# Rounding the third expert's high halves on VectorE instead of ScalarE, with three more slots for them

## The chip, the cores and the metric

The kernel runs on one core of one Trainium2 chip. The metric is the device time of one execution, in microseconds (us). Lower is better. Engines are named as in the profile: PE is TensorE (PEld its weight loads), DVE is VectorE, ACT is ScalarE, POOL is GpSimd, SP issues the DMAs.

## The reference, cut to what matters

The input x has the shape (32, 56, 56, 96), f32. Two residual layers follow each other:

```
x = x + attention(norm(x))         # shifted 7x7 windows, 12 heads, relative bias, masks
t = tokens of x
scores -> softmax over 4 experts, the best 2 kept and renormalised     # "masked"
h = gelu(norm(t) @ w1[e] + b1[e])      # e = 0..3, 96 -> 384
y = h @ w2[e] + b2[e]                  # 384 -> 96
out = t + sum over e of masked[e] * y[e]
```

All four experts are computed for all tokens; the gate sets two of them to zero. The change is in the second matmul of the experts, `h @ w2[e]`, and in how h is prepared for it.

## The kernel before

An image is cut into four units of 784 tokens (two strips of 7 by 56), 128 units in all. The 31 first images run in a loop whose body holds four units, the last image stands behind it. Each engine has a program of its own, written out by hand, and engines meet only at semaphores. The sequence within an engine is fixed by the code: nothing reorders it.

A step of the loop works on three units at once: f, whose expert layer is done; a, whose attention is done; b, whose norm, queries, keys and values are prepared. In f's first stretch, called the gelu stretch here, PE computes the hidden layer in 24 pieces (`hidden`), and ACT takes each through the gelu (`gelus`) into `g_sb`, 12 chunks of 128 hidden features by 784 tokens in f32. Three chunks make an expert. In the second stretch PE runs the attention of a in eight rounds n = 0 to 7 and puts the twelve groups of the experts' second matmul (`experts(f, g)`, three groups for each expert) in between: `GROUPS_AT` says which group stands in which round (0, 1, 2 in round 0, group 3 in round 1, 4 in round 2, 5 in round 3, 6 in round 5, 7 in round 6), and `LATE_GROUPS` those that follow the rounds.

The matmul reads h as two f16 halves. The high half `g_hi` is the rounded chunk, the low half `g_lo` is the difference between `g_sb` and it. Both have six slots, so that a chunk of the third or fourth expert takes the slot of a chunk of the first or second one, once `y_done` tells that its groups are through.

- Chunks 0 to 5: DVE rounds them in the gelu stretch (line 875), behind the router's arithmetic. The low halves of 0 to 2 are DVE's (line 880), those of 3 to 11 are POOL's (line 450).
- Chunks 6 to 11: ACT rounds them (line 536) in the rounds of the attention that the table `ROUND_AT` names: 6, 7, 8 in rounds 1, 2, 3, behind `copy_pt(n)` and `exps(n + 1)`.
- DVE's next work behind chunk 5 is `softmax_pair(a, 0)`: the maximum over the first scores (line 737) and their subtraction (line 741). ACT takes the exponential (line 560), PE transposes it (line 1038), ACT copies it to SBUF (line 565), PE multiplies it by the values (line 1055).
- POOL's program of a unit: low halves 3 to 5, three additions (line 460) of gated expert outputs to `xr`, the norm of b (lines 423, 428, 433), low halves 6 to 8 with an addition behind each, the others.

Groups 3 to 5 wait in PE for the low halves of chunks 3 to 5 (`lo_done`), groups 6 to 8 for those of chunks 6 to 8.

Of the kernel before, what the change touches and what calls it, by code (L numbers as in the profile page):

```python
# [28 lines left out]
F16 = mybir.dt.float16  # L29
ALU = mybir.AluOpType  # L30
ACT = mybir.ActivationFunctionType
AX = mybir.AxisListType

B, IMG, C = 32, 56, 96
# [7 lines left out]
CHUNKS = EXPERTS * HID // 128  # L42
CPE = HID // 128
UPI = 4
STRIP = W * IMG
TOK = 2 * STRIP
# [10 lines left out]
def at(unit, per_unit, k=0):  # L57

    m, c = unit
    return m * (UPI * per_unit) + (c * per_unit + k)  # L60
# [43 lines left out]
PARTS = len(GROUP_TILES)  # L104
# [1 line left out]
COMBINES_AT = ((0, 1), (2,), (3,), (4,), (5,), (), (6,), (7,))  # L106
LATE_GROUPS = (8, 9, 10, 11)
STATS_AT = ((), (0, 1), (2, 3), (4, 5, 6), (), (), (), ())
ROUND_AT = ((), (6,), (7,), (8,), (), (9,), (10,), (11,))


T1_AT = 4
# [11 lines left out]
N_XV = 8  # L124
N_PROJ, N_T2, N_H, N_Y = 2, 2, 24, PARTS * EXPERTS
N_XHI, N_X1LO = 4, 4
N_ROUND, N_LO = CHUNKS // 2, CHUNKS - CPE
PAD = 16
N_STACK = 16 * 3 * GROUPS
N_SPREAD = 16 * 3 * GH  # L130
# [10 lines left out]
def build(nc, x, packed, wp, consts, out, keys):  # L141
    ctx = ExitStack()
    with ctx:
        def sb(name, shape, dt=F32):
            return ctx.enter_context(nc.sbuf_tensor(name, shape, dt))
# [84 lines left out]
        gden = sb("gden", [LANES, W])  # L230
        gate = sb("gate", [LANES, W * EXPERTS])
        g_sb = sb("g_sb", [128, CHUNKS, TOK])
        g_hi = sb("g_hi", [128, 2 * CPE, TOK + PAD], F16)
        g_lo = sb("g_lo", [128, 2 * CPE, TOK + PAD], F16)
        y_gated = sb("y_gated", [LANES, 4, 3 * C])

# [172 lines left out]
        def _(pool):  # L409
# [32 lines left out]

            def low_part(f, chunk):

                if chunk < 2 * CPE:
                    pool.wait_ge(hi_dve, at(f, N_ROUND, chunk + 1))
                else:
                    pool.wait_ge(hi_act, at(f, N_ROUND, chunk - 2 * CPE + 1))
                slot = chunk % (2 * CPE)
                nc.gpsimd.tensor_tensor(g_lo[:, slot, 0:TOK], g_sb[:, chunk, :], g_hi[:, slot, 0:TOK],  # L450
                                        ALU.subtract).then_inc(lo_done, 1)

            def add(f, u, g):
# [40 lines left out]
        def _(act):  # L494
# [38 lines left out]
            def round_chunk(f, chunk):  # L533

                act.wait_ge(y_done, at(f, N_Y, PARTS * (chunk // CPE - 1)))
                nc.scalar.activation(g_hi[:, chunk - 2 * CPE, 0:TOK], g_sb[:, chunk, :], ACT.Copy  # L536
                                     ).then_inc(hi_act, 1)

            def gelus(f, k0):
# [75 lines left out]
            def step(f, a, b, u):  # L615
                for i in range(8):
                    gelus(f, 3 * i)
                    if i == 0:
                        router_tanh(f)
                if a is not None:  # L620
                    load_tables(ACT.Exp)
                    attention(a, b, f)
                else:
                    for chunk in range(2 * CPE, CHUNKS):
                        round_chunk(f, chunk)

            schedule(act, step, prologue)
# [3 lines left out]
        def _(dve):  # L631
# [310 lines left out]
            def step(f, a, b, u):  # L942
                router_b(f)
                for chunk in range(CPE):
                    round_chunk(f, chunk)
                for chunk in range(CPE):
                    low_part(f, chunk)
                for chunk in range(CPE, 2 * CPE):
                    round_chunk(f, chunk)
                if a is not None:  # L950
                    softmax_pair(a, 0)
                    attention(a, b, f)
                else:
                    for g in range(N_Y):
                        combine(f, g)
# [5 lines left out]
        def _(pe):  # L961
# [143 lines left out]
            def experts(f, g):  # L1105

                e, j0, n = tiles_of(g)
                if e == 0:
                    pe.wait_ge(lo_dve, at(f, CPE, CPE))
                else:  # L1110
                    pe.wait_ge(lo_done, at(f, N_LO, CPE * e))
                if g < 3:
                    pe.wait_ge(gelu_done, at(f, N_H, N_H - 2 + g))
                earlier = [i for i in range(g) if Y_BANK[i] == Y_BANK[g]]
                if earlier:
                    pe.wait_ge(gated, at(f, N_Y, max(earlier) + 1))
                y = y_bank(g)[:, 0:n * C]
                T.matmul(y, ones16[:, :], b2_16[:, e * 3 * C:e * 3 * C + n * C], start=True, stop=False,
                         skip_group_check=True)
                for k in range(n):  # L1120
                    cols = slice((j0 + k) * LANES, (j0 + k) * LANES + 128)
                    for c in range(CPE):
                        slot, wc = e % 2 * CPE + c, slice((e * CPE + c) * C, (e * CPE + c + 1) * C)
                        outp = y[:, k * C:(k + 1) * C]
                        T.matmul(outp, g_hi[:, slot, cols], w2_hi[:, wc], start=False, stop=False,  # L1125
                                 skip_group_check=True)
                        T.matmul(outp, g_hi[:, slot, cols], w2_lo[:, wc], start=False, stop=False,  # L1127
                                 skip_group_check=True)
                        ins = T.matmul(outp, g_lo[:, slot, cols], w2_hi[:, wc], start=False,  # L1129
                                       stop=(c == CPE - 1), skip_group_check=True)  # L1130
                ins.then_inc(y_done, 1)

# [145 lines left out]
```

## Time and profile before

| | |
|---|---|
| median of 3 runs | 6519.17 us (6518.93 to 6523.38) |
| the profiled execution, its own time | 6518.15 us |
| its span | 6516.3 us |
| granted TensorE clock | 0.995 |
| PE busy | 6280.1 us, 96% |
| DVE busy | 5032.7 us, 77% |
| ACT busy | 4717.1 us, 72% |
| POOL busy | 3756.0 us, 58% |

1.85 us of the time lie around the span. A unit takes some 50 us: the span over 128 units is 50.9. PE has the highest busy share, in all 40 slices of the span, but its records overlap and their ends are modelled, so that the share alone does not say that nothing else is waited for. In a row of the timeline, the figures are the start, the duration, and in brackets how long the engine had stood idle before it and what ended that. Rows that are merged (x3) can overlap: an instruction of DVE starts before the one ahead of it has ended.

### The profile page before, as it was taken

The page shows a single profiled execution, that of the slowest core. Times are in us where ns is not written, and L with a number is a line of the kernel's source. Part 1 is how long each engine was busy: PE and PEld are TensorE (multiplying, and loading weights), DVE is VectorE, ACT ScalarE, POOL GpSimd, SP SyncE. Part 2 cuts the span into 40 slices and gives each one's busy share as a digit, 9 for nine tenths or more (in the row PEclk, how much of TensorE's full clock was granted, in tenths as well). Part 3 has the DMA queues.
Part 4 walks back from the last instruction along what each step waited for, and adds up shares of the span by engine and source line. Part 5 has one row for each costly group of instructions (what it writes and reads, how often), then busy time and mean ns, then how long its engine had stood idle before and what let it go on. Part 6 is the DMA issues. An engine that isn't in the chain of part 4 may idle for free.

```text
span 6516.3 us, 265099 instructions
## 1 busy us (share of the span) xinstructions
PE 6280.1 (96%) x99456; PEld 5077.8 (78%) x99456; DVE 5032.7 (77%) x15655; ACT 4717.1 (72%) x9087; POOL 3756.0 (58%) x3337
## 2 busy tenths in 40 slices
PE   5999999999999999999999999999999999999998
PEld 4788778777877787778777877787787778777876
DVE  5777777777777777777777777777777777777775
ACT  3777777777777777777777777777777777777775
POOL 2565556555655565556556555655565556555655
PEclk9999999999999999999999999999999999999998
DMA  1111111111111111111111111111111111111110
GB/s 58 45 43 45 46 45 43 44 47 45 45 44 46 44 45 45 46 44 45 45 46 43 45 46 45 43 45 46 45 44 44 46 45 43 45 47 44 45 43 22
DMA packets 190611, 290.00 MB, mean 45 GB/s; under 512 B 42450, under 2 KB 151634, under 8 KB 189266
## 3 DMA queue, kind: packets, MB, share of 16 engines
q1 hardware_dynamic: 189394, 273.23, 14.5%
q8 instruction: 831, 13.62, 0.9%
q14 instruction: 386, 3.16, 0.2%
HBM read 138.18 MB, written 77.07 MB: 33 GB/s over the span
## 4 chain that ended last, share of the span: by engine, by line
PE 76%; DVE 13%; ACT 4%; issue 3%; POOL 2%; SPq 1%; DVEq 0%; DMA 0%; ACTq 0%; POOLq 0%
PE ps_t L1038 12%; PE ps_o L1055 10%; PE ps_f L966 8%; PE ps_f L967 8%; PE ps_f L968 8%; PE ps_s L1018 5%; PE ps_s L1028 4%; PE ps_f L1129 4%; PE ps_f L1127 4%; PE ps_f L1125 4%; POOL rstd L439 2%; PE ps_o L1064 2%; DVE stat L768 2%; PE ps_f L1070 2%; PE ps_t L985 2%
## 5 line engine op out<-in xcount | busy, mean ns | idle before, releaser
L450 POOL TENSOR_TENSOR g_lo<-g_sb,g_hi 128x784 f16<-128x784 f32 x1152 | 2013.5, 1756 | 1720.7 <-DVE g_hi L875 1019.1
L543 ACT ACTIVATE g_sb<-ps_f 128x392 f32<-128x392 f32 x3072 | 1525.5, 497 | 128.9 <-PE ps_f L968 127.8
L565 ACT ACTIVATE pt_sb<-ps_t 113x588 f32<-113x588 f32 x1024 | 676.2, 660 | 1011.2 <-PE ps_t L1038 998.2
L737 DVE TENSOR_REDUCE s_max<-ps_s 113x12 f32<-113x588 f32 x1024 | 789.2, 771 | 655.9 <-PE ps_s L1028 651.6
L1129 PE MATMUL ps_f<-w_hi,g_lo 128*128 128x96 f16 x8832 | 1229.1, 206 | 0.0
L1127 PE MATMUL ps_f<-w_lo,g_hi 128*128 128x96 f16 x8832 | 1228.5, 206 | 0.0
L1125 PE MATMUL ps_f<-w_hi,g_hi 128*128 128x96 f16 x8832 | 1227.9, 206 | 0.0
L460 POOL TENSOR_TENSOR xr<-y_gated,xr 112x192 f32<-112x192 f32 (+1 forms) x1536 | 985.3, 659 | 370.2 <-DVE y_gated L893 271.3
L966 PE MATMUL ps_f<-x_hi,w_hi 128*128 128x392 f16 x3072 | 1012.4, 330 | 19.8 <-issue 5.3
L967 PE MATMUL ps_f<-x_lo,w_hi 128*128 128x392 f16 x3072 | 1010.9, 329 | 0.0
L968 PE MATMUL ps_f<-x_hi,w_lo 128*128 128x392 f16 x3072 | 1010.9, 329 | 0.0
L1038 PE MATMUL ps_t<-ident,p_sb 113*113 113x113 f32 x6144 | 854.3, 275 | 26.8 <-ACT p_sb L560 26.6
L1127 PEld LDWEIGHTS ps_f<-w_lo,g_hi 128*128 128x128 f16 x8832 | 863.8, 98 | 10.3
L1125 PEld LDWEIGHTS ps_f<-w_hi,g_hi 128*128 128x128 f16 x8832 | 865.9, 98 | 0.1
L1129 PEld LDWEIGHTS ps_f<-w_hi,g_lo 128*128 128x128 f16 x8832 | 864.3, 98 | 0.0
L741 DVE TENSOR_TENSOR s_sub<-ps_s,s_max 113x588 f32<-113x588 f32 x1024 | 790.5, 772 | 57.0
L1055 PEld LDWEIGHTS ps_o<-v_bd,pt_sb 113*49 113x49 f32 x24576 | 737.5, 125 | 114.2 <-ACT pt_sb L565 67.0
L1055 PE MATMUL ps_o<-v_bd,pt_sb 113*49 113x18 f32 x24576 | 785.1, 198 | 23.9 <-ACT pt_sb L565 20.1
L560 ACT ACTIVATE p_sb<-s_sub 113x588 f32<-113x588 f32 x1024 | 715.6, 699 | 78.2 <-DVE s_sub L741 72.9
L1038 PEld LDWEIGHTS ps_t<-ident,p_sb 113*113 113x113 f32 x6144 | 695.6, 178 | 80.2 <-issue 51.3
L536 ACT ACTIVATE g_hi<-g_sb 128x784 f16<-128x784 f32 x768 | 647.0, 843 | 3.1 <-PE ps_f L1129 3.1
L439 POOL TENSOR_TENSOR rstd<-ve,cst 112x4 f32<-112x4 f32 (+1 forms) x256 | 270.6, 1057 | 596.6 <-DVE ve L777 596.6
(132 smaller groups left out, 13418.1 us busy)
## 6 DMA issues: line engine op xcount, KB each, us to landing
k_bd<-keys SPq DMA_DIRECT2D x1536, 36.8 KB
q_st<-qk_hi SPq DMA_DIRECT2D x768, 49.0 KB, 1.9
xr<-x SPq DMA_DIRECT2D x224, 139.1 KB
out<-xr SPq DMA_DIRECT2D x224, 139.1 KB
xa<-x SPq DMA_DIRECT2D x224, 136.5 KB
keys<-qk_hi SPq DMA_DIRECT2D x128, 147.0 KB, 2.4
keys<-qk_lo SPq DMA_DIRECT2D x128, 147.0 KB, 2.8
q_st<-qk_lo SPq DMA_DIRECT2D x384, 49.0 KB, 2.0
```

What stands on the lines that cost most here:

```text
L450: nc.gpsimd.tensor_tensor(g_lo[:, slot, 0:TOK], g_sb[:, chunk, :], g_hi[:, slot, 0:TOK], ALU.subtract).then_inc(lo_done, 1)
L460: nc.gpsimd.tensor_tensor(slot, y_gated[:, g % 4, 0:n * C], slot, ALU.add).then_inc(comb_done, 1)
L543: nc.scalar.activation(g_sb[:, chunk, half * STRIP:(half + 1) * STRIP], h_bank[k % 3][:, 0:STRIP], ACT.Gelu, scale=1.0 / WSCALE).then_inc( ...
L741: V.tensor_tensor(s_sub[:, n % 2, :, 0:WW], scores, s_max[:, :].unsqueeze(2).broadcast_to([SPAN, HEADS, WW]), ALU.subtract).then_inc(sub_d ...
L966: T.matmul(outp, lhs_hi, rhs_hi, start=start, stop=False, skip_group_check=True)
L967: T.matmul(outp, lhs_hi, rhs_lo, start=False, stop=False, skip_group_check=True)
L968: return T.matmul(outp, lhs_lo, rhs_hi, start=False, stop=True, skip_group_check=True)
L1038: ins = T.transpose(bank[2 + p // 4][0:SPAN, (p % 4) * 128:(p % 4) * 128 + SPAN], p_sb[0:SPAN, n % 2, 2 * p:2 * p + 2, :].rearrange("p h k ...
L1055: ins = T.matmul(ps_o[NB * s:NB * s + WW, O0 + p * 2 * VW:O0 + (p + 1) * 2 * VW], pt_sb[0:SPAN, p, s * WW:(s + 1) * WW], v_bd[0:SPAN, win ...
L1125: T.matmul(outp, g_hi[:, slot, cols], w2_hi[:, wc], start=False, stop=False, skip_group_check=True)
L1127: T.matmul(outp, g_hi[:, slot, cols], w2_lo[:, wc], start=False, stop=False, skip_group_check=True)
L1129: ins = T.matmul(outp, g_lo[:, slot, cols], w2_hi[:, wc], start=False, stop=(c == CPE - 1), skip_group_check=True)
```

## The change

DVE rounds chunks 6, 7 and 8 as well, behind chunk 5 and ahead of the first maximum. `g_hi` grows from six slots to nine, so that these three overwrite nothing that the first expert still reads; `g_lo` keeps six. ACT's table loses the entries of the chunks 6, 7 and 8, and chunks 9 to 11 now take the slots 0 to 2 of `g_hi`. POOL's low halves of 6 to 8 wait for DVE's rounding and, on their own now, for the groups of the expert whose `g_lo` slot they take. PE's and SP's programs have the same rows as before.

```diff
-ROUND_AT = ((), (6,), (7,), (8,), (), (9,), (10,), (11,))
+ROUND_AT = ((), (), (), (), (), (9,), (10,), (11,))
-N_ROUND, N_LO = CHUNKS // 2, CHUNKS - CPE
+N_ROUND, N_LO = 3 * CPE, CHUNKS - CPE
-        g_hi = sb("g_hi", [128, 2 * CPE, TOK + PAD], F16)
+        g_hi = sb("g_hi", [128, 3 * CPE, TOK + PAD], F16)
 # POOL, low_part
-                if chunk < 2 * CPE:
+                if chunk < 3 * CPE:
                     pool.wait_ge(hi_dve, at(f, N_ROUND, chunk + 1))
                 else:
-                    pool.wait_ge(hi_act, at(f, N_ROUND, chunk - 2 * CPE + 1))
+                    pool.wait_ge(hi_act, at(f, CPE, chunk - 3 * CPE + 1))
+                if chunk >= 2 * CPE:
+                    pool.wait_ge(y_done, at(f, N_Y, PARTS * (chunk // CPE - 1)))
                 slot = chunk % (2 * CPE)
-                nc.gpsimd.tensor_tensor(g_lo[:, slot, 0:TOK], g_sb[:, chunk, :], g_hi[:, slot, 0:TOK],
+                nc.gpsimd.tensor_tensor(g_lo[:, slot, 0:TOK], g_sb[:, chunk, :],
+                                        g_hi[:, chunk % (3 * CPE), 0:TOK],
                                         ALU.subtract).then_inc(lo_done, 1)
 # ACT, round_chunk
-                nc.scalar.activation(g_hi[:, chunk - 2 * CPE, 0:TOK], g_sb[:, chunk, :], ACT.Copy
+                nc.scalar.activation(g_hi[:, chunk - 3 * CPE, 0:TOK], g_sb[:, chunk, :], ACT.Copy
                                      ).then_inc(hi_act, 1)
 # ACT, step, last unit only
-                    for chunk in range(2 * CPE, CHUNKS):
+                    for chunk in range(3 * CPE, CHUNKS):
                         round_chunk(f, chunk)
 # DVE, step
-                for chunk in range(CPE, 2 * CPE):
+                for chunk in range(CPE, 3 * CPE):
                     round_chunk(f, chunk)
 # PE, experts: the same matmuls, other slots of g_hi
-                        slot, wc = e % 2 * CPE + c, slice((e * CPE + c) * C, (e * CPE + c + 1) * C)
+                        hi, lo = e % 3 * CPE + c, e % 2 * CPE + c
+                        wc = slice((e * CPE + c) * C, (e * CPE + c + 1) * C)
```

On DVE, in the loop's body between the low halves of the first expert and the first maximum of the attention, before:

```order
L880 TENSOR_TENSOR g_lo<-g_sb,g_hi 128x784 [waits hi_dve]
L874 REGISTER_ALU
L875 CAST g_hi<-g_sb 128x784 [waits gelu_done]
L874 REGISTER_ALU
L875 CAST g_hi<-g_sb 128x784 [waits gelu_done]
L874 REGISTER_ALU
L875 CAST g_hi<-g_sb 128x784 [waits gelu_done]
L736 ISA
L737 TENSOR_REDUCE s_max<-ps_s 113x12 [waits s_done]
L740 REGISTER_ALU [waits max_done]
L741 TENSOR_TENSOR s_sub<-ps_s,s_max 113x12x49 [waits exp_done]
```

The same place after:

```order
L878 REGISTER_ALU
L879 CAST g_hi<-g_sb 128x784 [waits gelu_done]
L878 REGISTER_ALU
L879 CAST g_hi<-g_sb 128x784 [waits gelu_done]
L878 REGISTER_ALU
L879 CAST g_hi<-g_sb 128x784 [waits gelu_done]
L740 ISA
L741 TENSOR_REDUCE s_max<-ps_s 113x12 [waits s_done]
L744 REGISTER_ALU [waits max_done]
L745 TENSOR_TENSOR s_sub<-ps_s,s_max 113x12x49 [waits exp_done]
```

The casts shown last are those of the chunks 6, 7 and 8; three like them, of 3 to 5, stand ahead of them. Six casts in a row now stand ahead of the first maximum where there were three.

On ACT, in rounds 1 and 2 of the attention, before:

```order
L565 ACTIVATE pt_sb<-ps_t 113x588 [waits pt_done]
L554 REGISTER_ALU
L560 ACTIVATE p_sb<-s_sub 113x12x49 [waits pt_done,sub_done]
L535 REGISTER_ALU
L536 ACTIVATE g_hi<-g_sb 128x784 [waits y_done]
L564 REGISTER_ALU
L565 ACTIVATE pt_sb<-ps_t 113x588 [waits pt_done]
```

and after:

```order
L569 ACTIVATE pt_sb<-ps_t 113x588 [waits pt_done]
L558 REGISTER_ALU
L564 ACTIVATE p_sb<-s_sub 113x12x49 [waits pt_done,sub_done]
L568 REGISTER_ALU
L569 ACTIVATE pt_sb<-ps_t 113x588 [waits pt_done]
```

The rounding is gone from between the exponential of one round and the copy of the next one.

## Rows read from the trace of the kernel before

**Rows 1.** The page's chain that ended last, by engine.
```profile
PE 76%; DVE 13%; ACT 4%; issue 3%; POOL 2%; SPq 1%; DVEq 0%; DMA 0%; ACTq 0%; POOLq 0%
```

**Rows 2.** Waits: engine, tile, line <- releaser: us in total, times, longest.
```profile
PE ps_t L1038 <- ACT p_sb L560: 26.6, 125, 1.1
PE ps_o L1055 <- ACT pt_sb L565: 20.1, 128, 0.6
```

**Rows 3.** ACT's timeline in rounds 1 to 4 of a unit.
```profile
3032.27 0.70 ACT L560 ACTIVATE p_sb<-s_sub 113x588 f32<-113x588 f32 x1
3032.86 0.84 ACT L536 ACTIVATE g_hi<-g_sb 128x784 f16<-128x784 f32 x1
3034.76 0.66 ACT L565 ACTIVATE pt_sb<-ps_t 113x588 f32<-113x588 f32 x1 [1.05 <-PE ps_t L1038]
...
3037.64 0.66 ACT L565 ACTIVATE pt_sb<-ps_t 113x588 f32<-113x588 f32 x1 [0.90 <-PE ps_t L1038]
...
3040.94 0.66 ACT L565 ACTIVATE pt_sb<-ps_t 113x588 f32<-113x588 f32 x1 [1.32 <-PE ps_t L1038]
```

**Rows 4.** Groups by line, ACT and DVE: count, busy us, mean ns, idle before.
```profile
L536 ACT ACTIVATE g_hi<-g_sb 128x784 f16<-128x784 f32 x768 | 647.0, 843 | 3.1 <-PE ps_f L1129 3.1
...
L875 DVE CAST g_hi<-g_sb 128x784 f16<-128x784 f32 x768 | 388.9, 563 | 16.3
L880 DVE TENSOR_TENSOR g_lo<-g_sb,g_hi 128x784 f16<-128x784 f32 x384 | 350.7, 969 | 0.0
```

**Rows 5.** DVE's timeline from the casts to the first subtraction, same unit.
```profile
3018.45 2.74 DVE L880 TENSOR_TENSOR g_lo<-g_sb,g_hi 128x784 f16<-128x784 f32 x3
3021.10 1.51 DVE L875 CAST g_hi<-g_sb 128x784 f16<-128x784 f32 x3
3025.03 0.77 DVE L737 TENSOR_REDUCE s_max<-ps_s 113x12 f32<-113x588 f32 x1 [2.41 <-PE ps_s L1028]
3025.92 0.77 DVE L741 TENSOR_TENSOR s_sub<-ps_s,s_max 113x588 f32<-113x588 f32 x1
```

**Rows 6.** The chain from the first scores to the first transpose, same unit.
```profile
3025.03 0.78 DVE s_max L737
3025.87 0.04 issue
3025.92 0.78 DVE s_sub L741
3026.76 0.05 issue
3026.81 0.71 ACT p_sb L560
3027.52 0.14 issue
3027.65 0.82 PE ps_t L1038 x6
```

**Rows 7.** DVE's first maximum, the units with the shortest and longest idle.
```profile
326.73 0.77 DVE L737 TENSOR_REDUCE s_max<-ps_s 113x12 f32<-113x588 f32 x1 [2.16 <-PE ps_s L1028]
...
6426.79 0.77 DVE L737 TENSOR_REDUCE s_max<-ps_s 113x12 f32<-113x588 f32 x1 [2.69 <-PE ps_s L1028]
```

**Rows 8.** ACT's gelus of the same unit.
```profile
3014.45 10.44 ACT L543 ACTIVATE g_sb<-ps_f 128x392 f32<-128x392 f32 x21
```

**Rows 9.** POOL's low halves 3, and 4 and 5, same unit.
```profile
3021.74 2.41 POOL L450 TENSOR_TENSOR g_lo<-g_sb,g_hi 128x784 f16<-128x784 f32 x1 [7.88 <-DVE g_hi L875]
...
3024.11 3.31 POOL L450 TENSOR_TENSOR g_lo<-g_sb,g_hi 128x784 f16<-128x784 f32 x2
```

**Rows 10.** POOL's additions behind them, in the unit with the shortest idle.
```profile
2322.55 5.69 POOL L450 TENSOR_TENSOR g_lo<-g_sb,g_hi 128x784 f16<-128x784 f32 x3 [8.45 <-DVE g_hi L875]
2330.07 1.90 POOL L460 TENSOR_TENSOR xr<-y_gated,xr 112x192 f32<-112x192 f32 x3 [1.83 <-DVE y_gated L893]
```

**Rows 11.** PE at the start of group 3, round 1.
```profile
3031.51 0.25 PE L1118 MATMUL ps_f<-b,ones 128*128 128x192 f16 x1
```

**Rows 12.** POOL's timeline in the last unit.
```profile
6474.68 5.67 POOL L450 TENSOR_TENSOR g_lo<-g_sb,g_hi 128x784 f16<-128x784 f32 x3 [7.75 <-DVE g_hi L875]
6480.31 1.89 POOL L460 TENSOR_TENSOR xr<-y_gated,xr 112x192 f32<-112x192 f32 x3
6482.16 1.67 POOL L450 TENSOR_TENSOR g_lo<-g_sb,g_hi 128x784 f16<-128x784 f32 x1
...
6494.32 0.59 POOL L460 TENSOR_TENSOR xr<-y_gated,xr 112x192 f32<-112x192 f32 x1
6495.36 1.34 POOL L460 TENSOR_TENSOR xr<-y_gated,xr 112x288 f32<-112x288 f32 x2 [0.45 <-DVE y_gated L893]
...
6498.33 0.79 POOL L460 TENSOR_TENSOR xr<-y_gated,xr 112x288 f32<-112x288 f32 x1 [0.78 <-DVE y_gated L893]
```

More of the change, by code:

```diff
@@ L1122, in experts @@
                     for c in range(CPE):
-                        slot, wc = e % 2 * CPE + c, slice((e * CPE + c) * C, (e * CPE + c + 1) * C)
+                        hi, lo = e % 3 * CPE + c, e % 2 * CPE + c
+                        wc = slice((e * CPE + c) * C, (e * CPE + c + 1) * C)
                         outp = y[:, k * C:(k + 1) * C]
-                        T.matmul(outp, g_hi[:, slot, cols], w2_hi[:, wc], start=False, stop=False,
+                        T.matmul(outp, g_hi[:, hi, cols], w2_hi[:, wc], start=False, stop=False,
                                  skip_group_check=True)
-                        T.matmul(outp, g_hi[:, slot, cols], w2_lo[:, wc], start=False, stop=False,
+                        T.matmul(outp, g_hi[:, hi, cols], w2_lo[:, wc], start=False, stop=False,
                                  skip_group_check=True)
-                        ins = T.matmul(outp, g_lo[:, slot, cols], w2_hi[:, wc], start=False,
+                        ins = T.matmul(outp, g_lo[:, lo, cols], w2_hi[:, wc], start=False,
                                        stop=(c == CPE - 1), skip_group_check=True)
```

## The prediction, on record before the result was known

> **What bounds the kernel now.** I read the chain that ended last first: 76% of it is PE, 13% DVE, 4% ACT [rows 1]. ACT loses work by this change, so the question is whether any of its 4% lies where the roundings stood. The table of waits comes next: PE stood idle for ACT's exponential 26.6 us and for ACT's copy 20.1 us, each about once in a unit (125 and 128 times) [rows 2]. Then the timeline of one unit shows where. The reader is to see two things in it. In rounds 1 to 3 it is ACT that waits for PE: behind each rounding it stands idle 1.05, 0.90 and 1.32 us before PE's transposes release it [rows 3]. And at the first scores, ahead of round 0, the chain runs over DVE and ACT with no gap to speak of: maximum, subtraction, exponential, transposes, from 3025.03 to 3027.65 [rows 6]. There a microsecond on DVE is a microsecond of the unit, and that is the place in front of which the change puts its three casts.
>
> **The change part by part.**
>
> ACT loses 3 roundings in each of 128 units, 384 x 0.843 = 323.7 us busy [rows 4]. All of it lies beside PE's work: if the rounding goes, ACT's idle time behind it grows from 0.90 to 1.32 us to some 1.7 to 2.2 us, and the copy starts when it started before. Gain on the path: nothing. The upper bound of a gain is what PE waits for ACT at all, 26.6 + 20.1 = 46.7 us [rows 2]; but the first of these waits is the transpose of round 0 (3027.65, behind the chain of rows 6), where no rounding stood ahead, and the second one's count is one in a unit where six or more roundings are done. I take 0 and keep 46.7 as the far end of a gain.
>
> DVE gets 3 casts in each unit. Their form is that of the other six: 563 ns each [rows 4], and three of them in 1.51 us, so one every (1.51 - 0.56)/2 = 0.475 us [rows 5]. Three more are 1.43 us in a row. Their input: 21 gelus run from 3014.45 to 3024.89, one every 0.497 us, behind three earlier ones [rows 8]. Chunks 6, 7 and 8 need 14, 16 and 18 gelus: done at 3014.45 + 11, 13, 15 x 0.497 = 3019.9, 3020.9 and 3021.9. DVE is free for them at 3022.53, 3023.00 and 3023.48, so none waits. The last ends at 3022.61 + 1.43 = 3024.04, and the first maximum, which waits for PE's scores, starts at 3025.03 [rows 5]. Cover: DVE's idle time of 2.41 us there, of which 0.98 is left. It is not the same in each unit: of the 127 first maxima that follow the casts the idle time is 2.16 at the least and 2.69 at the most [rows 7], their sum is 310.6 us (mean 2.45). In the worst, 0.73 us is left. Cost: 0. If the cover were gone, each missing 0.1 us would be 0.1 x 127 = 12.7 us.
>
> The bounds of a cast here: 0.475 us a piece from below, the row of the same operation; from above the nearest slower row on DVE of the same size, the low half, three in 2.74, one every (2.74 - 0.97)/2 = 0.885 us [rows 4, 5]. Three of those are 2.66 us: 0.50, 0.25 and 0.07 us too many for the units with an idle time of about 2.16 (30 units), 2.41 (32) and 2.59 and more (65). Sum 15.0 + 8.0 + 4.6 = 27.6 us. I take the lower bound, since operation, types and shape are its own and slots 6 to 8 lie at the same stride as the others.
>
> POOL pays for the casts, though it has no new work. Its low half of chunk 3 takes 2.41 us beside the casts of chunks 4 and 5, while the next two take 3.31 us together [rows 9]. Counted back from its end (3024.15) by the undisturbed 1.67 us [rows 12], it did its work from 3022.48 on, which is when DVE was through with its last cast (3022.61 less the overlap). With three casts more in the same row, POOL is held until 3022.48 + 1.43 = 3023.9, and its low halves end at 3027.42 + 1.43 = 3028.85. Who waits: group 3 of the experts starts at 3031.51 [rows 11], 2.66 us later; the additions wait for DVE anyway, 1.83 us at the least, so 0.40 us is left to them [rows 10]. Behind them POOL's program runs as before, and low half 6 starts when the norm of b is done, not when its rounding is. Cost in the loop: 0.
>
> The last unit is the one place where POOL is on the path. Its rows follow each other without a gap from 6474.68 to 6494.9, and the additions and groups behind them hang on the last low half [rows 12]. ACT's roundings are not awaited there (low half 6 starts as the additions end), so their removal gives nothing, and POOL's delay shifts everything to the end: +1.43 us. Lower bound 0, if the waits further down take up some of it.
>
> The other edits go together: POOL's added wait for `y_done` names groups that are done before (ACT waited for the same ones), and what stands behind it is an addition that was behind it already; three more slots' margins in one memset of the setup; PE and SP run the rows that they ran. Cost 0.
>
> Sum against the profiled execution: 6518.15 + 0 (ACT) + 0 (DVE) + 0 (POOL in the loop) + 1.43 (last unit) = 6519.6 us. The median of the runs shown, 6519.17, lies 1.0 above that execution, so the two differ by no more than runs do. The span should be 6516.3 + 1.4 = 6517.7.
>
> What the Trainium skill says of this place ("SBUF — State Buffer", section "Who interferes with whom"): a cast in a two-port mode and a GpSimd instruction hold the port pair that they share for a whole instruction, and the one that issues first blocks the other fully. The trace agrees that POOL is blocked, by 2.41 - 1.67 = 0.74 us. It does not agree on who goes first: POOL's low half had started at 3021.74, ahead of the cast of chunk 5, and DVE's cast took its 0.56 us all the same (768 casts, mean 563 ns). By the page's rule one of the three new casts should find POOL in possession; by the row none does.
>
> **The rivals.**
>
> *POOL gets the port between two casts (slower).* The mechanism: POOL's waiting low half gets in at the gap behind chunk 5's cast, and DVE's next cast waits until it is through. Price: 1.67 us of delay for DVE, with 2.45 - 1.43 = 1.02 us of cover on the mean: 0.65 us late in each of 127 units, 82.6 us, and the time is 6601. It decides from the point where DVE's casts end later than PE's first scores, because exponential and transposes follow at once [rows 6]. If it happened before each new cast: 3 x 1.67 = 5.0 us against 1.02, 3.99 x 127 = 506 us, 7025. For it: POOL is pending during the whole row of casts. Against it: it was pending during the step from chunk 4's cast to 5's as well, in every unit, and lost there each time. It is also what the Trainium skill's page on SBUF would have. Chance 0.07.
>
> *The casts are as slow as the low halves (slower).* 6518.15 + 27.6 + 1.4 = 6547. For it: the longer row of casts runs beside work that the old ones did not see, the last gelus' writes to `g_sb` above all. Against it: the casts of 3 to 5 ran beside gelus and POOL and kept their duration. Chance 0.03.
>
> *ACT's relief is worth something (faster).* If PE's waits for the copy came from ACT being late by its roundings, they would go: 6518.15 - 20.1 + 1.4 = 6499.5, at most 6518.15 - 46.7 + 1.4 = 6473. For it: 20.1 us in 128 waits. Against it: rounds 1 to 3 have 0.90 us and more of idle time on ACT behind the rounding [rows 3]. Chance 0.03.
>
> **How the numbers follow.** Forecast 0.87, rivals 0.07, 0.03 and 0.03. The likeliest time is 6519.6. Within 0.2%, which is 13 us here (6506 to 6532) and about what a measurement of this kernel can tell from no change, lies the forecast: same 0.87. Slower 0.10, faster 0.03. The range: the forecast's own reaches from 6512 (0.05 us gained in each unit, an eighth of what PE waits for ACT) to 6528 (the highest of the runs shown, 6523.4, and 0.04 us lost in each unit); with it some 0.05 of the forecast and 0.13 of the rivals are left out.
>
> **What would show each step.** In the profile after: line 536's group has 384 instructions and DVE's cast 1152 at 0.56 us; DVE's idle time before the first maximum is 0.7 to 1.3 us instead of 2.16 to 2.69; POOL's low half 3 takes about 3.8 us instead of 2.41, and its idle time before the first additions falls by 1.4; ACT stands idle 1.7 us and more in rounds 2 to 4; POOL's last addition starts 1.4 us later against the span's start. The prediction is wrong if a cast lasts 2 us (POOL got in), if the first maximum follows a cast directly, or if PE's waits for `p_sb` grow or those for `pt_sb` vanish.

## The result and the profile after

| | before | after |
|---|---|---|
| median (4 runs each) | 6521.07 us | 6557.10 us |
| lowest and highest | 6518.93, 6523.38 | 6555.52, 6563.12 |
| span of the profiled execution | 6516.3 us | 6555.4 us |
| granted TensorE clock | 0.995 | 0.996 |
| DVE, ACT, POOL busy | 5032.7, 4717.1, 3756.0 | 5210.3, 4427.5, 3939.2 |

The ratio is 1.0059, interval 1.0047 to 1.0071: slower by 0.6%, outside the range of 6512 to 6528. The prediction was wrong.

First, the rows on which it rested. The groups by line, after (line, engine, operation, output and inputs, count, then busy us and mean ns, then idle before):

```profile
L453 POOL TENSOR_TENSOR g_lo<-g_sb,g_hi 128x784 f16<-128x784 f32 x1152 | 2196.7, 1916 | 1722.4 <-DVE g_hi L879 1022.7
...
L879 DVE CAST g_hi<-g_sb 128x784 f16<-128x784 f32 x1152 | 572.3, 563 | 16.3
...
L540 ACT ACTIVATE g_hi<-g_sb 128x784 f16<-128x784 f32 x384 | 323.7, 843 | 6.9 <-PE ps_f L1134 6.9
```

ACT did 384 roundings less at 843 ns, DVE 384 casts more at 563 ns, as worked out from [rows 4]. The timeline of DVE in one unit, after:

```profile
3139.86 2.95 DVE L879 CAST g_hi<-g_sb 128x784 f16<-128x784 f32 x6
3144.11 0.77 DVE L741 TENSOR_REDUCE s_max<-ps_s 113x12 f32<-113x588 f32 x1 [1.30 <-PE ps_s L1032]
```

and POOL's in the same unit:

```profile
3140.50 7.11 POOL L453 TENSOR_TENSOR g_lo<-g_sb,g_hi 128x784 f16<-128x784 f32 x3 [9.02 <-DVE g_hi L879]
```

Six casts take 2.95 us where three took 1.51 [rows 5]: 1.44 more. The first maximum still waits for PE, by 1.30 us here. POOL's three low halves take 7.11 us where they took 5.67 to 5.69 [rows 10, 12]. All of this is as forecast. What is new stands in the page's chain that ended last:

```profile
PE 75%; DVE 12%; issue 5%; ACT 4%; POOL 2%; SPq 1%; DVEq 0%; ACTq 0%; DMA 0%; POOLq 0%
```

"issue" was 3% [rows 1] and is 5% now: time in which an engine of the chain waited for nothing that the profile shows. To find its place I took the length of each unit, from one first maximum to the next, in both traces. DVE's first maxima in two units in a row, with the loop's branch between them, before:

```profile
3074.91 0.77 DVE L737 TENSOR_REDUCE s_max<-ps_s 113x12 f32<-113x588 f32 x1 [2.59 <-PE ps_s L1028]
...
3125.12 0.77 DVE L737 TENSOR_REDUCE s_max<-ps_s 113x12 f32<-113x588 f32 x1 [2.17 <-PE ps_s L1028]
```

and after:

```profile
3092.65 0.77 DVE L741 TENSOR_REDUCE s_max<-ps_s 113x12 f32<-113x588 f32 x1 [1.16 <-PE ps_s L1032]
...
3144.11 0.77 DVE L741 TENSOR_REDUCE s_max<-ps_s 113x12 f32<-113x588 f32 x1 [1.30 <-PE ps_s L1032]
```

50.21 us before, 51.46 after. The median of all of them, by place in the loop's body of four units (31 or 32 units each):

| | first | second | third | fourth, over the loop's branch |
|---|---|---|---|---|
| before | 49.89 | 49.89 | 49.89 | 50.21 |
| after | 49.89 | 50.17 | 49.89 | 51.21 |

The first and the third unit take what they took, with the same casts and the same delay of POOL in them. Summed over the trace: the fourth units grew by 32.1 us, the second ones by 7.7, the first and third together shrank by 1.9; the stretch behind the last maximum grew by 2.6 and the one ahead of the first shrank by 1.4. That is 39.1, the whole difference of the spans.

**The fourth unit.** The chain there, after (start, us, what; a "q" behind the engine's name is its sequencer, the part that reads the instructions, waits and branches):

```profile
3129.21 0.04 ACT x_hi L530
3129.25 0.32 issue
3129.57 0.05 ACTq L308
3129.62 2.38 issue
3132.00 0.03 ACTq L308
...
3132.26 0.51 ACT g_sb L547
3132.76 0.05 issue
3132.81 0.34 PE ps_f L970
```

Line 308 is the loop itself, `nc.Fori(..., hint_back_edge=True)`. Its rows around that branch, for ACT and DVE (duration min/median/max in ns, first and last start):

```profile
L308 ACTq COMPARE_BRANCH  x1: 49/49/49, 3129.6 to 3129.6; - x1
...
L308 ACTq BRANCH_PREFETCH_HINT  x1: 31/31/31, 3132.0 to 3132.0; - x1
...
L308 DVEq COMPARE_BRANCH  x1: 68/68/68, 3132.3 to 3132.3; - x1
L308 DVEq BRANCH_PREFETCH_HINT  x1: 39/39/39, 3132.8 to 3132.8; - x1
```

ACT branches back at 3129.6, and the first instruction of the body, the hint row, runs at 3132.0; the median over the 30 branches that go back is 2.18 us. DVE needs 0.53. The same two rows before:

```profile
L308 ACTq COMPARE_BRANCH  x1: 49/49/49, 3111.4 to 3111.4; - x1
L308 ACTq BRANCH_PREFETCH_HINT  x1: 31/31/31, 3111.8 to 3111.8; - x1
```

0.41 us at the median. Who waits, after (engine, tile, line <- releaser: us in total, times, longest):

```profile
ACT g_sb L547 <- PE ps_f L972: 160.7, 227, 2.7
...
DVE gden L856 <- ACT gtanh L554: 31.2, 30, 1.3
...
PE ps_f L970 <- ACT g_sb L547: 22.0, 30, 1.0
```

PE's hidden layer has no free PSUM tile until the gelus begin: 30 waits of up to 1.0 us for `g_sb` that were not there before. The first row names PE as the releaser of gelus; at this place the chain above shows ACT standing without an instruction instead, so a releaser that the profile infers can be the wrong one.

**The second unit.** DVE's second scaling of the norm, `xn`, waits for POOL's `rstd`. Chain after:

```profile
3026.79 1.11 POOL rstd L439
3027.90 0.03 issue
...
3027.95 0.40 issue
3028.35 0.47 DVE xn L792
```

and at the same place before:

```profile
3009.34 1.11 POOL rstd L439
...
3010.49 0.04 issue
3010.54 0.46 DVE xn L788
```

`rstd` is ready in both; DVE's instruction starts 0.45 us behind it instead of 0.10.

No cast and no rounding of the change runs at either place. What the two share is that an engine stands with its inputs ready. The page counts DMA packets of kind "instruction" in two queues, 831 of 16 KB in one and 386 (before) or 388 (after) of 8 KB in the other. I took as theory 1 that the changed length of ACT's and DVE's programs moves the places at which their instruction stream is interrupted (from the trace's counts, a turn of the body is 527 instructions on ACT before and 511 after, 782 and 806 on DVE; POOL's grew too, from 231 to 267, but its time from the branch to the first row is 0.21 us in both), theory 2 that ACT's missing roundings shift it badly, theory 3 that the casts, or POOL's delay by them, are what costs.

The trace also has the start of every instruction packet, and that is where theory 1 can be seen directly. In the stretch from 3129.6 to 3131.0, after, in which ACT stands at the branch:

```profile
q14 instruction: 1, 0.01, 1.4%
```

and before, from 3110.6 until ACT is through with the branch at 3111.8:

```profile
DMA packets 0, 0.00 MB, mean 0 GB/s; under 512 B 0, under 2 KB 0, under 8 KB 0
```

Read for every turn, an 8 KB packet starts 0.65 to 1.00 us behind ACT's branch (median 0.67) in all 30 turns after, and ACT's first row follows a good microsecond behind its landing. Before, none starts between the branch and the first row in any turn: the nearest one ahead of the branch lies 7.4 us from it. At the late `xn`, such a packet starts 0.67 us behind the late row in 31 of the 32 turns, and in none before. In DVE's program, before, the rows at which such packets start follow each other at a distance of 126 to 129: so 8 KB hold some 128 instructions, 64 bytes each.

### The profile page after: what moved, and what is told of

Read it like the earlier page. It is cut to its first block, busy times and chain, and to the rows that moved or that the text cites. A ratio compares the mean times of both kernels' runs of the same rounds, so it can differ in the third digit from the quotient of the medians.

```text
span 6555.4 us, 266487 instructions
## 1 busy us (share of the span) xinstructions
PE 6282.3 (96%) x99456; PEld 5072.1 (77%) x99456; DVE 5210.3 (79%) x16039; ACT 4427.5 (68%) x8703; POOL 3939.2 (60%) x3337
## 4 chain that ended last, share of the span: by engine, by line
PE 75%; DVE 12%; issue 5%; ACT 4%; POOL 2%; SPq 1%; DVEq 0%; ACTq 0%; DMA 0%; POOLq 0%
PE ps_t L1042 12%; PE ps_o L1059 10%; PE ps_f L970 8%; PE ps_f L971 8%; PE ps_f L972 8%; PE ps_s L1022 5%; PE ps_s L1032 4%; PE ps_f L1132 3%; PE ps_f L1134 3%; PE ps_f L1130 3%; POOL rstd L439 2%; PE ps_o L1068 2%; DVE stat L772 2%; PE ps_f L1074 2%; PE ps_t L989 2%
## 5 line engine op out<-in xcount | busy, mean ns | idle before, releaser
L453 POOL TENSOR_TENSOR g_lo<-g_sb,g_hi 128x784 f16<-128x784 f32 x1152 | 2196.7, 1916 | 1722.4 <-DVE g_hi L879 1022.7
L1042 PE MATMUL ps_t<-ident,p_sb 113*113 113x113 f32 x6144 | 854.0, 275 | 25.8 <-ACT p_sb L564 25.5
L1059 PE MATMUL ps_o<-v_bd,pt_sb 113*49 113x18 f32 x24576 | 784.5, 199 | 24.0 <-ACT pt_sb L569 20.1
L879 DVE CAST g_hi<-g_sb 128x784 f16<-128x784 f32 x1152 | 572.3, 563 | 16.3
```

Of the source, the lines that this page charges most:

```text
L1042: ins = T.transpose(bank[2 + p // 4][0:SPAN, (p % 4) * 128:(p % 4) * 128 + SPAN], p_sb[0:SPAN, n % 2, 2 * p:2 * p + 2, :].rearrange("p h k ...
L1059: ins = T.matmul(ps_o[NB * s:NB * s + WW, O0 + p * 2 * VW:O0 + (p + 1) * 2 * VW], pt_sb[0:SPAN, p, s * WW:(s + 1) * WW], v_bd[0:SPAN, win ...
```

## The experiments

Line numbers shift by a few lines between the kernels. A filler is an instruction of one element that touches nothing else; unless said otherwise it stands ahead of the loop, so that it runs once and only shifts the program behind it. "Gap" is the time from an engine's branch to its first instruction in the body (median of 30; before: ACT 0.41, DVE 0.53), and the four lengths are those of the table above. ACT's own instruction packet at the branch, where one is named, is its start against the branch.

### e1 and e2: the changed kernel with ACT's stream filled up

e1 puts a 1x1 activation where each rounding stood; e2 leaves the body alone and puts 16 fillers ahead of the loop.

```diff
 # e1: the changed kernel, ACT round_chunk
-ROUND_AT = ((), (), (), (), (), (9,), (10,), (11,))
+ROUND_AT = ((), (6,), (7,), (8,), (), (9,), (10,), (11,))
+                if chunk < 3 * CPE:
+                    nc.scalar.activation(spare_a[:, chunk:chunk + 1], cst[0:1, 4:5], ACT.Copy)
+                    return
 # e2: the changed kernel, ACT's prologue
+                for k in range(16):
+                    nc.scalar.activation(spare_a[:, k:k + 1], cst[0:1, 4:5], ACT.Copy)
```

> The changed kernel, with a 1x1 activation (0.2 us) on ACT in each place where a rounding of chunks 6 to 8 stood, so that ACT's loop body has as many instructions as before the change (498 instead of 482) while ACT still does not do the work. Its output is the changed kernel's. Theory 1 (instruction supply): the 1.2 us that ACT stands without an instruction behind the loop's branch comes from where the end and the start of ACT's body lie in the blocks in which instructions are fetched; with the old length it goes, 31 x 1.0 = 31 us, and some 8.7 us stay (31 x 0.28, DVE's late instruction in the second unit of the body): 6521 + 9 = 6530 us. Theory 2 (ACT's missing work): the stall comes from ACT doing less in rounds 1 to 3; it stays, 6557 us. Theory 3 (DVE's casts or POOL's delay reach the edge of the loop): 6557 us.

> The changed kernel with 16 one-element activations ahead of ACT's wait for the setup, where ACT is idle for 47 us. The loop is untouched; it only lies 16 instructions further on, so that its end (not its start) lies where that of the kernel before lies. Theory 1: if the end's place decides, the stall at the branch goes and the time is about 6530 us; if the start's place decides it may stay. Theories 2 and 3: nothing in the loop has changed, 6557 us.

Measured: e1 6532.26 us, ratio to before 1.0022 (1.0012 to 1.0032); e2 6531.85, 1.0021 (1.0011 to 1.0031). Units in e2 49.89, 50.18, 49.89, 50.38, in e1 the same within 0.01; ACT's gap 0.41 in both. So 25 us go away by 16 instructions outside the loop, with all computation as in the changed kernel. No packet starts in the gap any more, in any turn. Theory 2 falls: in e2 ACT's roundings are missing and it costs nothing. In both, the waits of PE and the gate's division for ACT are back to what they were: the row of e2 is

```profile
DVE xn L796 <- POOL rstd L440: 67.7, 128, 0.8
...
DVE gden L860 <- ACT gtanh L555: 19.6, 30, 0.7
```

with `gden` at 19.6 us instead of 31.2, while the wait of `xn` stays at 67.7 (before: 56.5 in 128 waits, the longest 0.4). The second unit is untouched, so it is not ACT's.

### e3: the kernel before with 112 fillers on ACT

```diff
 # the kernel before, ACT's prologue
+                for k in range(112):
+                    nc.scalar.activation(spare_a[:, k:k + 1], cst[0:1, 4:5], ACT.Copy)
```

> The kernel before with 112 one-element activations ahead of ACT's wait for the setup, so that the loop's end lies, modulo 128 instructions (8 KB, the size of the instruction packets in the trace), where that of the changed kernel lies. No instruction of the loop is changed. Theory 1: the stall at the branch appears, 6521 + 31 = 6552 us. Theories 2 and 3: as the kernel before, 6521 us.

Measured: 6518.03 us, ratio 0.9999 (0.9990 to 1.0009), units 49.89, 49.89, 49.89, 50.21, gap 0.41. A miss. The fillers put the end of ACT's body where the changed kernel has it, counted modulo 128 rows, and no stall came: the end's place alone does not decide. Nor does the start's, which is the same in the kernels before and after. ACT's last packet ahead of the branch is still some 7 us away from it.

### e4: ACT's part alone

The kernel before without the roundings of chunks 6 to 8; nobody makes these high halves, and the third expert reads old ones. POOL's low halves of 6 to 8 wait for `y_done` themselves, as in the changed kernel.

```diff
 # the kernel before
-ROUND_AT = ((), (6,), (7,), (8,), (), (9,), (10,), (11,))
+ROUND_AT = ((), (), (), (), (), (9,), (10,), (11,))
```

> The kernel before without ACT's roundings of chunks 6 to 8 and with nothing in their place: the third expert reads what the first one left in its slots of g_hi. DVE as before. ACT's body has the changed kernel's length. Theories 1 and 2: 6521 + 31 = 6552 us, with ACT without an instruction for over 2 us behind the loop's branch. Theory 3: 6521 us, or less.

Measured: 6547.89 us, ratio 1.0045 (1.0029 to 1.0062), units 49.89, 49.89, 49.89, 51.24, ACT's gap 2.33, with ACT's packet at 0.67 us behind the branch. Waits:

```profile
ACT g_sb L545 <- PE ps_f L970: 166.1, 227, 2.9
DVE xn L790 <- POOL rstd L439: 56.7, 128, 0.4
...
DVE gden L854 <- ACT gtanh L552: 34.6, 30, 1.5
```

Work taken away from ACT, none added anywhere, and the kernel is 0.45% slower. The stall at the branch comes with ACT's half of the change and the one at `xn` does not. The idle time before the first maximum is no shorter than before (medians of the four units 2.42 to 2.73 us, before 2.17 to 2.59), and POOL's three low halves take 5.68 us as before, so neither casts nor POOL have a part in it.

### e6: DVE's part alone

```diff
 # the kernel before: three casts more, into slots that nobody reads
-        g_hi = sb("g_hi", [128, 2 * CPE, TOK + PAD], F16)
+        g_hi = sb("g_hi", [128, 3 * CPE, TOK + PAD], F16)
+                for chunk in range(2 * CPE, 3 * CPE):
+                    dve.wait_ge(gelu_done, at(f, N_H, gelus_of(chunk)))
+                    V.tensor_copy(g_hi[:, chunk, 0:TOK], g_sb[:, chunk, :])
```

> The kernel before with three more casts on DVE behind chunk 5's, into three slots of g_hi that nothing reads; ACT still rounds chunks 6 to 8 for the matmuls. ACT's program is as before, DVE's has the changed kernel's 6 rows more in each unit. Theory 1: no stall of ACT at the loop's branch; DVE's late instruction in the second unit of the body is there as in the changed kernel or a little off it, 31 x 0.45 = 14 us at most, so 6519 to 6533 us. A theory that puts the whole 39 us on DVE: 6557 us.

Measured: 6530.72 us, ratio 1.0019 (1.0010 to 1.0028), units 49.88, 50.17, 49.88, 50.37, ACT's gap 0.41, and the wait for `rstd`:

```profile
DVE xn L788 <- POOL rstd L439: 67.8, 128, 0.8
```

The second stall comes with DVE's half. It costs 0.28 us in the second unit and 0.16 in the fourth, 32 x 0.28 + 31 x 0.16 = 13.9 us, nearly all of the difference of 14.3 to the runs before beside it (6516.47). It could still be the casts themselves, and that is what e5 and e8 are for.

### e5: the changed kernel with both streams shifted

16 fillers on ACT as in e2 and 116 on DVE.

```diff
 # the changed kernel, DVE's prologue (ACT's as in e2)
+                for k in range(116):
+                    V.memset(spare_d[:, k:k + 1], 0.0)
```

> The changed kernel with 16 one-element activations ahead of ACT's wait for the setup and 116 one-element memsets at the start of DVE's program, both while these engines wait for the first DMAs; the loop is untouched and lies further on in both programs. 116 is chosen so that no multiple of 128 instructions of DVE's program falls between the statistics of the residual and the low half of its normalised tokens, or at the first maximum, of any of the four units. Theory 1 (instruction supply): both late instructions go, each unit takes what it took before the change, and the time is 6518 + 1.4 (last unit) = 6519 to 6521 us. Theory 4 (what is left after ACT's rows are moved, 14 us, comes from the casts themselves or from POOL held by them): 6532 us as with ACT's rows moved alone.

Measured: 6523.46 us, ratio 1.0011 (1.0002 to 1.0020), units 50.00, 49.88, 49.88, 50.21, gaps 0.41 and 0.53:

```profile
DVE xn L797 <- POOL rstd L441: 56.7, 128, 0.4
...
DVE gden L861 <- ACT gtanh L556: 19.6, 30, 0.7
```

Both stalls are gone, and both waits stand where they stood before. Second, third and fourth unit take to 0.01 us what they take in the kernel before, though DVE makes six casts in a row and POOL is held in each of them; the first takes 49.89 in the changed kernel itself. Theory 3 falls: what the casts and POOL's delay cost in the loop is 0. A rest of 0.11 us in the first unit, 32 x 0.11 = 3.5 us, is half of the remaining 7 us. It too is an instruction that comes late: `o_tok` (line 761) starts 0.12 us later in that unit than before, and in 30 of 31 turns a packet starts 0.67 us behind it; in the kernel before and in e9, where the unit takes 49.89 and 49.88, none does.

### e8: the kernel before with 10 fillers on DVE

> The kernel before with 10 one-element memsets at the start of DVE's program, which is idle there. They put the instruction that scales the second part of the normalised residual in the second unit of the loop's body at the place in DVE's program (the 506th row) where it stands in the changed kernel. Theory 1: this instruction comes 0.36 us late and the second of the four units takes 50.17 us instead of 49.89, 31 x 0.28 = 8.7 us in all: 6527 us. If the change's own work makes it late: 6518 us and 49.89 us.

Measured: 6529.48 us, ratio 1.0018 (1.0009 to 1.0027), units 49.88, 49.88, 49.88, 50.57. A late instruction came, but not in the second unit, and it costs more than the 8.7 us expected: it is in the fourth, 31 x 0.36 = 11.2 us.

```profile
DVE xn L789 <- POOL rstd L440: 42.9, 97, 0.4
...
DVE x_lo L817 <- ACT x_hi L527: 13.4, 33, 0.8
DVE xn L789 <- issue: 8.7, 31, 0.3
```

31 times `xn` waits for nothing that the profile shows, and in 30 turns a packet starts 0.7 us behind it. In the second unit the packet starts, in most turns, 1.1 us behind an `xn` that is on time: ten rows missed the place there by little and hit one in the fourth unit. Ten one-element instructions that run once, in a kernel without a single change in its loop, cost 13 us: that is as much as DVE's half of the change.

### e7, e10 and e11: other shifts of the kernel before on ACT

240, 100 and 106 fillers, as in e3 (those of e7 read another idle tile).

> The kernel before with 240 one-element activations ahead of ACT's wait for the setup. The loop's end then lies, modulo 256 instructions (and not only modulo 128), where that of the changed kernel lies. No instruction of the loop is changed. Theory 1 with blocks of 256 instructions: ACT stands without an instruction for over 2 us behind the loop's branch and the time is 6518 + 31 = 6549 us. If the block were 128 instructions or the place of the loop's start decided alone, it would stay at 6518 us, as with 112.

> The kernel before with 100 one-element activations ahead of ACT's wait for the setup. With 112 and with 240 the last of ACT's fetches in the body stayed 7 us ahead of the branch, and nothing was late. Theory 1: a place exists at which that fetch falls behind the last table load, close to the branch; then ACT stands for some 2 us behind the branch and the time is 6518 + 31 = 6549 us. If 100 rows are not that place, 6518 us.

> The kernel before with 106 one-element activations ahead of ACT's wait for the setup, another place for the same loop. As with 100: 6549 us if ACT's last fetch of the body falls next to the branch, 6518 us otherwise; nothing in between but a second, small stall of up to 0.3 us in a unit.

Measured: e7 6515.65 us, ratio 0.9999 (0.9989 to 1.0008); e10 and e11, one run each, 6515.65 and 6514.43. No gap above 0.41, fourth unit 50.20 to 50.21 in all three: misses. For the longer body I found no shift that brings ACT's stall about. The packets say why these four tell little: ACT's last one ahead of the branch starts 7.4 us ahead of it in e3 and e7 and some 45 us in e10 and e11. None of them put a packet at the branch, so that a bad shift may well exist and was not hit.

### e9: both streams shifted, DVE's by 100

> The changed kernel with 16 one-element activations on ACT, as before, and 100 one-element memsets on DVE instead of 116. With 116, three of the four units took what they took before the change, and the first of the body 50.00 us instead of 49.89. Theory 1: those 0.11 us are again a fetch of DVE's that falls on the path, and move or go with the 16 rows; the time is 6518 to 6524 us and no unit is late by more than 0.3 us. Theory 4 (the casts or POOL's delay cost it): the 0.11 us stay in the first unit.

Measured: 6536.46 us, ratio 1.0030 (1.0019 to 1.0042), units 49.88, 49.89, 49.89, 50.76. The 0.11 us of the first unit are gone, and a stall at the branch has come up, now DVE's (gap 1.67):

```profile
DVE xn L797 <- POOL rstd L441: 56.6, 128, 0.4
...
DVE gden L861 <- issue: 54.8, 30, 2.1
```

The chain there:

```profile
3123.58 0.07 DVEq L310
3123.65 1.66 issue
3125.32 0.04 DVEq L310
```

16 rows less than in e5 cost 13 us. Here DVE's packet starts within 0.2 us of its branch, on either side, in all 30 turns; in e5 none does. The first maximum of that unit follows the casts with no idle time at all: DVE is late by 1.14 us, and e5 has 0.75 us of idle time left there. So in this kernel the three casts are no longer covered. In the other three units the changed work costs nothing, as in e5.

### e12 to e16: how far the changed kernel's stall at the branch reaches

64, 4, 8, 128 and 256 fillers on ACT alone, one run each. What was open: whether the stall depends on where the body stands within a packet of 8 KB, 128 instructions. Then shifts by 128 and 256 change nothing, and small ones take it away.

> The changed kernel with 64 one-element activations ahead of ACT's wait for the setup. Theory 1: the stall at the branch is a matter of place, and 64 rows from it (half of a packet's 128) ACT's last fetch falls tens of us ahead of the branch: no stall, 6532 us as with 16. If any length of 511 rows with a start other than 16 further on stalls: 6557 us.

> The changed kernel with 4 one-element activations ahead of ACT's wait for the setup. In the changed kernel ACT's last fetch starts within 1 us of the branch. Theory 1: 4 rows earlier in the body it falls on the row of the last gelu input's copy, still under 2 us ahead of the branch: the stall stays, whole or in part, 6540 to 6557 us. If the bad place is narrower than 4 rows: 6530 us.

> The changed kernel with 8 one-element activations there. Theory 1: the last fetch then falls at the table load, 5 us ahead of the branch: no stall, 6530 us. If the bad place is wider than 8 rows: 6557 us.

> The changed kernel with 128 one-element activations there, one 8 KB packet of instructions. Theory 1 with a period of 128 rows: the same place again, so the stall is back and the time is 6557 us. With a longer period: 6530 us.

> The changed kernel with 256 one-element activations there, two packets (16 KB). Theory 1 with a period of 128 or 256 rows: the stall is back, 6557 us (256 of these activations take 24 us and end before ACT's first work). If the place matters in another way than modulo 256: 6530 us.

| fillers on ACT | 0 | 4 | 8 | 16 (e2) | 64 | 128 | 256 |
|---|---|---|---|---|---|---|---|
| time, us | 6557.1 | 6536.1 | 6536.3 | 6531.9 | 6529.8 | 6564.5 | 6559.1 |
| ACT's gap, us | 2.18 | 1.29 | 0.41 | 0.41 | 0.41 | 2.26 | 2.27 |
| ACT's packet at the branch, us | +0.67 | -0.21 | none | none | none | +0.66 | +0.66 |
| fourth unit, us | 51.21 | 50.37 | 50.37 | 50.38 | 50.37 | 51.28 | 51.29 |

The stall goes within eight rows and comes back at 128 and 256. The times are single runs but for 0 and 16, and what lies ahead of the loop and behind it differs by some us between them; the gap and the fourth unit are medians over the turns and decide. With four fillers the gap is 0.88 us too long and costs nothing. So about 0.9 us of ACT's delay are covered there, and of the changed kernel's 1.77 us (2.18 - 0.41) some 0.84 come through (51.21 - 50.37). What is left above the 50.21 of before, 0.16 us, is the fourth unit's part of DVE's half (e6), which is in all seven kernels.

The Trainium skill says of this place ("Runtime: NRT & Kernel Launch", section "Instruction fetch mechanics") that an engine's instruction memory is small and refilled in order, and that a taken branch to a page outside of it has to wait for a fetch. The gap of 2.18 us beside 0.41 agrees with a fetch that is sometimes waited for; packets of 8 KB, and a period of 128 and not 256 rows, are what the runs here show in place of its 16 KiB blocks. The same section calls the crossing of a boundary in sequence "mostly hidden". The late `xn` does not bear that out for a row on the chain: 0.35 us, 32 times. That it is such a crossing is shown by two things together: shifting the rows moves or removes it (e5, e8), and a packet starts 0.67 us behind the late row (31 of 32 turns), and none there in the kernel before.

## Why the prediction was wrong

**The step that failed** is in the first and the last of the change's parts: "Gain on the path: nothing" for ACT's loss of 3 roundings, with the bound drawn only on the side of a gain, and "PE and SP run the rows that they ran. Cost 0", which asks after the rows of the two engines that have none changed and not after those of ACT and DVE. DVE's part, "Cost: 0", has the same lack. All three price an instruction by the engine's time alone; the sum has no term for the changed length of ACT's and DVE's programs. Their measured prices: ACT's half of the change +29.8 us alone (e4: 6547.89 - 6518.11; its fourth units give 31 x 1.03 = 31.9) and +25.3 beside DVE's (6557.10 - 6531.85, e2), DVE's half +14.3 (e6). 25.3 + 14.3 = 39.6; measured together 36.0 by the medians and 39.1 by the two traces. In both halves the place, not the work, makes the price: 16 fillers take ACT's away (e2), 116 DVE's (e5).

**ACT's relief worth nothing as work**: right. PE's waits for the exponential and for the copy are 25.5 and 20.1 us after, against 26.6 and 20.1 [rows 2]. The rival of a gain is out.

**Three casts in 1.43 us, hidden**: right, by row and by price. Of the 2.16 to 2.69 us of idle time [rows 7], 1.16 and 1.30 are left in the units shown; in e5, with neither stall, the median at the branch is 0.75, where 0.73 was worked out as the worst (one unit, the first, has 0.35). In e9, where DVE's branch stalls, this cover is used up. The rivals "POOL gets the port" and "casts as slow as low halves" are out: 1152 casts at a mean of 563 ns, six of them in 2.95 us. (The prices of the first, 6601 and 7025, left out the 1.4 us of the last unit, which changes nothing.) Of the rule in the Trainium skill ("SBUF — State Buffer", "Who interferes with whom") the trace again shows the blocking and not who goes first: POOL's low half starts at 3140.50, inside the row of casts, and they take 2.95 us all the same.

**POOL held 1.43 us longer, hidden in the loop**: right. 7.11 us for three low halves instead of 5.67 to 5.69, and three of the four units of e5 are as long as before.

**The last unit +1.43**: right in its own place; what it adds up to at the end is not resolved. POOL's rows there, after:

```profile
6511.19 7.10 POOL L453 TENSOR_TENSOR g_lo<-g_sb,g_hi 128x784 f16<-128x784 f32 x3 [7.76 <-DVE g_hi L879]
...
6532.25 0.59 POOL L464 TENSOR_TENSOR xr<-y_gated,xr 112x192 f32<-112x192 f32 x1
6533.94 0.79 POOL L464 TENSOR_TENSOR xr<-y_gated,xr 112x288 f32<-112x288 f32 x1 [1.10 <-DVE y_gated L897]
...
6537.28 0.79 POOL L464 TENSOR_TENSOR xr<-y_gated,xr 112x288 f32<-112x288 f32 x1 [0.78 <-DVE y_gated L897]
```

From the first low half to the last addition without a wait it is 21.06 us against 19.64 [rows 12], +1.42; to the last addition of all 26.09 against 23.65, +2.44. The part beyond 1.43 goes along with TensorE's clock, which stands at the lower of its two levels (0.50, 1.2 GHz) behind the low halves. The stretch in which it comes back, after (us, then busy us and count of each engine, PEclk, DMA share, GB/s):

```profile
6531.00:6533.00 2.00, 2.00 (x26) 2.00 (x25) 0.00 (x0) 0.00 (x0) 1.84 (x2) 0.50 0.00 0
6533.00:6535.00 2.00, 2.00 (x37) 1.99 (x35) 0.81 (x2) 0.00 (x0) 0.79 (x1) 0.74 0.00 0
```

It comes back some 23 us behind the first low half; before, the stretch from 6493 to 6495, some 19 us behind it, shows 0.76. But the change is not needed for that: in e4, where POOL is not held, the distance to the last addition is 25.13 us, and in e3, with the loop and the last unit of the kernel before untouched, 25.21, with the clock back after 22.5 us; in e7 it is 23.77. So this end moves by 1.5 us between executions of the same work, and a delay of 1.43 cannot be read from it.

**What remains open.** A bad shift for the longer body: the four tried on ACT put no packet at the branch. What `hint_back_edge=True` of the loop does: every kernel here has it, and none was run without. Why a packet beside the branch costs a microsecond or two, while one that another engine's program needs at the same moment costs nothing (after, ACT's packet starts 0.1 us behind DVE's branch, and DVE's gap stays 0.53). And some 3.5 of the 7 us (interval 1 to 13) by which e5 still stands above before; the last unit's 1.43 may be among them. Among the versions that do the changed work, none beat the kernel before.

## What to carry to other kernels

In a kernel whose engines run programs of their own in a loop, each edit changes the length of a program, and with it where the loop stands in the instruction stream; here that was worth 0.45% in one half and 0.2% in the other half of an edit whose work cost nothing. Before believing a difference under 1%, compare the time from each engine's branch to its first instruction in the body and the "issue" pieces of the chain in both traces, look whether an instruction packet starts beside them, and measure the new version with a few one-element instructions ahead of the loop. If the time follows these fillers, the edit has not been measured yet.

## What the runs showed of the hardware

- Removing 384 activations of 843 ns made the kernel slower by 0.45% (e4).
- A loop's branch costs ACT 0.41 us or 2.2 us, depending on 8 instructions that run once ahead of the loop; the pattern repeats after 128 (e14, e15). On DVE it is 0.53 or 1.67 us (e5, e9).
- ACT's gap is long exactly where an 8 KB instruction packet starts between 0.3 us ahead of its branch and its first row behind it: in 30 of 30 turns each of after, e4, e13, e15 and e16, and in no turn of the thirteen other kernels, before among them. DVE's long gap in e9 has such a packet in 30 of 30 turns too.
- An instruction in the middle of the body can start 0.35 us late with all its inputs there, in every turn of the loop (after, e6, e8); an instruction packet starts 0.7 us behind it.
- Ten fillers on DVE, run once, cost 13 us in all (e8).
